# Attention scores and maxima as products over 64 rows, issued in couples on the two row halves of TensorE's array

## What is computed

```
q = split_heads(x @ Wq + bq, 16); k = split_heads(x @ Wk + bk, 16); v = split_heads(x @ Wv + bv, 16)
pattern = jnp.einsum('bhid,bhjd->bhij', k, q) * scale      # 2048 x 2048 for each of 2 x 16 heads
prob = jax.nn.softmax(pattern, axis=-2)                    # over the keys i, for each query j
out = jnp.einsum('bhis,bhid->bhsd', prob, v)
```

## Time and profile before

| | |
|---|---|
| median of 3 runs | 4837.88 us (4835.5 to 4839.3) |
| profiled execution, its own time | 4833.63 us |
| span of the profiled execution | 4831.8 us |
| TensorE busy | 4504.0 us, 93% of the span |
| VectorE busy | 3447.5 us, 71% |
| GpSimd busy | 2736.8 us, 57% |
| ScalarE busy | 2191.5 us, 45% |

### The profile page before, as it was taken

How to read it: one execution, slowest core, us unless ns; L and a number is a source line. 1 busy time by engine, 2 the same in 40 slices (tenths; PEclk the granted TensorE clock), 3 DMA queues, 4 the chain that set the end, 5 groups by cost and what they waited for, 6 DMA issues and landing times.

```text
span 4831.8 us, 57873 instructions
## 1 busy us (share of the span) xinstructions
PE 4504.0 (93%) x21400; PEld 2750.5 (57%) x21400; DVE 3447.5 (71%) x4562; ACT 2191.5 (45%) x3523; POOL 2736.8 (57%) x1202
## 2 busy tenths in 40 slices
PE   7999999999999999999999999858999896989898
PEld 5555555555555555555555555426777665767575
DVE  6888878878788788787888887465655454566455
ACT  5434444434444444444444444315565443555442
POOL 3666656566555565565565666705666233666432
PEclk9999999999999999999999999979999998999999
DMA  2000000000000000000000000010000100000001
GB/s 65 1 5 4 2 5 1 5 5 1 5 4 2 5 1 5 5 1 5 4 2 5 3 2 2 1 57 1 0 1 1 36 1 18 1 1 1 1 1 35
DMA packets 58327, 36.26 MB, mean 8 GB/s; under 512 B 33684, under 2 KB 56168, under 8 KB 58088
## 3 DMA queue, kind: packets, MB, share of 16 engines
q1 hardware_dynamic: 58088, 33.02, 2.4%
HBM read 28.54 MB, written 4.19 MB: 7 GB/s over the span
## 4 chain that ended last, share of the span: by engine, by line
POOL 48%; issue 26%; PE 11%; DVE 8%; ACT 4%; POOLq 1%; DMA 0%; DVEq 0%; SPq 0%; ACTq 0%
POOL accp L738 36%; POOL lp L760 4%; PE psum L1627 3%; POOL accp L734 3%; PE psum L1756 2%; POOL rnorm L750 2%; POOL qk_u L755 2%; PE psum L1769 2%; DVE ssq L1227 1%; ACT lp L941 1%; PE psum L1673 1%; ACT qk_sq L925 1%; DVE qk_w L1239 1%; POOL ug_l L788 1%; DVE lneg L1253 1%
## 5 line engine op out<-in xcount | busy, mean ns | idle before, releaser
L738 POOL TENSOR_TENSOR accp<-accp,prob 128x1024 f32<-128x1024 f32 x640 | 1593.7, 2490 | 712.1 <-ACT prob L895 675.1
L895 ACT ACTIVATE prob<-psum 128x1024 f32<-128x1024 f32 x1024 | 1041.4, 1025 | 1559.6 <-PE psum L1478 1400.0
L1124 DVE TENSOR_REDUCE mx<-psum 128x1 f32<-128x512 f32 x1984 | 1276.3, 684 | 383.9 <-PE psum L1449 338.5
L1489 PE MATMUL psum<-prob,vv 128*64 128x512 f32 x4096 | 991.6, 605 | 0.0
L1477 PE MATMUL psum<-qhh,klh 128*128 128x512 f32 x2048 | 826.1, 403 | 14.0 <-DVE klh L1087 11.8
L1478 PE MATMUL psum<-qlm,kh 65*128 65x512 f32 x2048 | 814.0, 397 | 0.0
L1449 PE MATMUL psum<-klh,qhh 128*128 128x512 f32 x1984 | 710.1, 419 | 30.5 <-DVE mx L1124 27.2
L1449 PEld LDWEIGHTS psum<-klh,qhh 128*128 128x128 f32 x1984 | 346.3, 189 | 430.6 <-DVE mx L1124 272.2
L1489 PEld LDWEIGHTS psum<-prob,vv 128*64 128x64 f32 x4096 | 248.4, 136 | 511.3 <-issue 433.6
L1477 PEld LDWEIGHTS psum<-qhh,klh 128*128 128x128 f32 x2048 | 390.4, 191 | 178.3 <-issue 69.7
L1147 DVE TENSOR_TENSOR accd<-accd,prob 128x1024 f32<-128x1024 f32 x192 | 421.6, 2196 | 22.5 <-ACT prob L895 21.3
(11 more groups left out here) (194 smaller groups left out, 6451.4 us busy)
## 6 DMA issues: line engine op xcount, KB each, us to landing
rot_l<-const_rot SPq DMA_DIRECT2D x2, 2048.0 KB, 8.7
out<-lpT SPq DMA_DIRECT2D x32, 128.0 KB, 1.7
wqkv_l<-L_ffn_wqkv SPq DMA_DIRECT2D x4, 768.0 KB, 9.7
w_l<-L_ffn_w SPq DMA_DIRECT2D x4, 618.0 KB
wqk<-L_attn_Wq SPq DMA_DIRECT2D x32, 64.0 KB, 2.0
wqk<-L_attn_Wk SPq DMA_DIRECT2D x32, 64.0 KB, 2.0
wv_p<-L_attn_Wv SPq DMA_DIRECT2D x16, 128.0 KB, 2.2
wo_p<-L_attn_Wo SPq DMA_DIRECT2D x16, 128.0 KB, 2.0
```

The lines of the kernel that those rows point to most:

```text
L738: pool.tensor_tensor(acc_p[cp][:], first[:], prob[kt % PRING][:], ALU.add).then_inc(pool_sum, 1)
L895: act.activation(prob[t % PRING][:], psum[:, S_BANK + 2 * (t % 2):S_BANK + 2 * (t % 2) + 2, :].rearrange("p a b -> p (a b)"), ACT.Exp, sca ...
L1124: dve.tensor_reduce(mx4[:, j // CHUNKS, j % CHUNKS:j % CHUNKS + 1], ps, AX_X, ALU.max).then_inc(ring_free, 1)
L1489: mm = pe.matmul(psum[j * DH:(j + 1) * DH, O_BANK, :], vv[:, kt, s * DH:(s + 1) * DH], prob[t % PRING][:, j * T:(j + 1) * T], start=(kt == ...
```

## The change

The operands of a head are laid out anew. Of the four chunks of 512 queries or keys, chunks 0 and 2 have their queries in rows 0 to 63 (e = 0), chunks 1 and 3 in rows 64 to 127 (e = 1). `qh` and `ql` (128 x 1024) hold high and low queries, `kh` and `kl` (128 x 2048) high and low keys in both row halves. Three blocks of weights (Wq, Wk, Wq) let one projection over 128 columns put queries above keys or keys above queries.

A step's scores are four couples of products, each couple one product over rows 0 to 63 for the one block of queries and one over rows 64 to 127 for the other: `one`.`nm` (ones in one row, the negated maxima), `kh`.`qh`, `kl`.`qh` and `kh`.`ql`. The maxima are `kh`.`qh` alone, without the low keys, also as a couple: 32 couples in a head in place of 64 products. VectorE still reduces 64 tiles. A couple takes two banks of the ring at once.

The second copy of the high keys is written by ScalarE, in place of its second copy of the high queries; that of the low keys by two transfers on SyncE's queue (`double_low`), for which TensorE waits at the start of the head (`kl_in`). VectorE's copy of the high keys (L1085) is gone. The negated maxima go into `nm` by two transfers. More weights and biases are loaded.

```diff
-            return [-(-RING_MAX * sum(weight[:g + 1]) // sum(weight)) for g in range(GROUPS)]
+            return [-(-COUPLES * sum(weight[:g + 1]) // sum(weight)) for g in range(GROUPS)]
...
-                tiles = [("max", j) for j in range(done, upto)]
+                couples = [("max", k) for k in range(done, upto)]
+                head = couples[:-1][:1]
+                middle = couples[1:-1]
+                tail = couples[-1:]
                 if g in outs:
-                    tiles += [("out", 2 * (g - 1)), ("out", 2 * (g - 1) + 1)]
+                    tail += [("out", 2 * (g - 1)), ("out", 2 * (g - 1) + 1)]
...
-                    order += tiles[:cut0] + [("scores", 2 * g + 2)] + tiles[cut0:cut1] + [("scores", 2 * g + 3)] + tiles[cut1:]
+                    order += head + [("scores", 2 * g + 2)] + middle + [("scores", 2 * g + 3)] + tail
...
+            def double_low(G, s):
+
+                sp.wait_ge(pj_dve, G * QK_ITEMS + QK_ITEMS)
+                for e in range(2):
+                    to, src = (kl[s][half(o), :].bitcast(F32).rearrange("p (c e n) -> p c e n", e=2, n=T)[:, :, e, :] for o in (e, 1 - e))
+                    sp.dma_start(to, src).then_inc(kl_in[s], 16)
...
-                    act.activation(qhh[s][DH:P, cols], qhh[s][0:DH, cols], ACT.Copy).then_inc(pj_dup, 1)
+                    act.activation(kh[s][q, cols], kh[s][k, cols], ACT.Copy).then_inc(pj_dup, 1)
...
-                dve.tensor_copy(kh1[s][0:DH, cols], klh[s][DH:P, cols])
-                dve.scalar_tensor_tensor(qlm[s][0:DH, cols], ps[0:DH], bqk_h[s][0:DH, 0:1], qhh[s][0:DH, cols], ALU.add, ALU.subtract)
-                dve.scalar_tensor_tensor(klh[s][0:DH, cols], ps[DH:P], bqk_h[s][DH:P, 0:1], klh[s][DH:P, cols], ALU.add, ALU.subtract).then_inc(pj_dve, 1)
+                dve.scalar_tensor_tensor(ql[s][q, pair_cols], ps[q], bqk_h[s][q, e:e + 1], qh[s][q, pair_cols], ALU.add, ALU.subtract)
+                dve.scalar_tensor_tensor(kl[s][k, cols], ps[k], bqk_h[s][k, e:e + 1], kh[s][k, cols], ALU.add, ALU.subtract).then_inc(pj_dve, 1)
...
-            def max_tile(rb, i, j):
-                ps = ring_wait(rb, i)
-                dve.tensor_reduce(mx4[:, j // CHUNKS, j % CHUNKS:j % CHUNKS + 1], ps, AX_X, ALU.max).then_inc(ring_free, 1)
+            def max_couple(rb, r, k):
+                qt, c = divmod(k, CHUNKS)
+                for e in range(2):
+                    ps = ring_wait(rb, r + e)
+                    dve.tensor_reduce(mx4[:, e, qt, c:c + 1], ps, AX_X, ALU.max).then_inc(ring_free, 1)
...
-                pe.matmul(ps, qhh[s][:, qt * P:(qt + 1) * P], klh[s][:, c * T:(c + 1) * T],
-                          start=True, stop=True).then_inc(ring_full, 1)
+            def couple_product(banks, s, k):
+
+                qt, c = divmod(k, CHUNKS)
+                for e in range(2):
+                    mm = pe.matmul(banks[e], qh[s][half(e), qt * P:(qt + 1) * P], kh[s][half(e), c * T:(c + 1) * T], start=True, stop=True)
+                return mm
+
+            def max_couple(rb, r, s, k):
+
+                couple_product([ring_slot(rb, r + e) for e in range(2)], s, k).then_inc(ring_full, 2)
...
-                for j in range(2):
-                    cols = slice((2 * cp + j) * T, (2 * cp + j + 1) * T)
-                    ps = psum[:, S_BANK + 2 * (t % 2) + j, :]
-                    pe.matmul(ps, klh[s][:, keys], qhh[s][:, cols], start=True, stop=False)
-                    mm = pe.matmul(ps, kh1[s][:, keys], qlm[s][:, cols], start=False, stop=True)
+                cols = slice(cp * T, (cp + 1) * T)
+                parts = ((one[:], nm[s]), (kh[s][:, keys], qh[s]), (kl[s][:, keys], qh[s]), (kh[s][:, keys], ql[s]))
+                for n, (left, right) in enumerate(parts):
+                    for e in range(2):
+                        mm = pe.matmul(psum[:, S_BANK + 2 * (t % 2) + e, :], left[half(e)], right[half(e), cols],
+                                       start=(n == 0), stop=(n == len(parts) - 1))
                 mm.then_inc(s_full, 1)
...
-                    pe.wait_ge(mrow, G * 16 + 32)
+                    pe.wait_ge(mrow, G * 32 + 64)
+                    pe.wait_ge(kl_in[s], p * 32 + 32)
```

More of the change, by code:

```diff
@@ L265, in adaln_block @@
         pj_full, pj_hi, pj_dup, pj_dve = sem("pj_full"), sem("pj_hi"), sem("pj_dup"), sem("pj_dve")
+        kl_in = [sem(f"kl_in{s}") for s in range(2)]
         ring_full, ring_free = sem("ring_full"), sem("ring_free")
@@ L355, in places @@
                 return 2 if j == TWINS - 1 else 1
-            return int(kind in ("max", "sum", "out", "proj_v"))
+            if kind == "max":
+                return 2
+            return int(kind in ("sum", "out", "proj_v"))
         def pair_plan(which):
@@ L376, in place, with half, couple_columns @@
             return [r for k, _, r in PLAN[which][hh] if k == kind][-1]
+        def half(e):
+            return slice(e * DH, (e + 1) * DH)
+        def couple_columns(i):
+            return slice(i // 2 * T, (i // 2 + 1) * T)
         def head_index(p, hh):
@@ L635, in _ @@
             pair(ALL_PAIRS - 1, True, PAIRS - 1, None, LAST)
-            sp.wait_ge(mrow, 16 + 16 * HEADS * B)
+            sp.wait_ge(mrow, 32 + 32 * HEADS * B)
+            for s in range(2):
+                sp.wait_ge(kl_in[s], 32 * ALL_PAIRS)
             sp.sem_inc(bar_left, 1)
@@ L701, in _ @@
             for s in range(2):
[L702 to L703 removed]
+                pool.memset(nm[s][:].bitcast(F32), 0.0).then_inc(cst, 1)
+            pool.memset(one[:].bitcast(F32), 0.0).then_inc(cst, 1)
+            pool.wait_ge(cst, 4)
+            for e in range(2):
+                pool.memset(one[e * DH:e * DH + 1, :].bitcast(F32), 1.0).then_inc(cst, 1)
+            pool.wait_ge(cst, 6)
             pool.sem_inc(pool_sum, OFF_POOL)
@@ L1547, in first_maxima @@
                     pe.wait_ge(pm_free, k - 1)
-                qt, c = divmod(2 * k, CHUNKS)
-                for j in range(2):
-                    mm = pe.matmul(psum[:, 4 + 2 * (k % 2) + j, :], qhh[0][:, qt * P:(qt + 1) * P], klh[0][:, (c + j) * T:(c + j + 1) * T],
-                                   start=True, stop=True)
-                mm.then_inc(pm_full, 1)
+                couple_product([psum[:, 4 + 2 * (k % 2) + e, :] for e in range(2)], 0, k).then_inc(pm_full, 1)
             def first_values(i):
```

84 lines of the change are left out of this document (44 added, 40 removed).

## The result

| | before | after |
|---|---|---|
| median of 4 runs | 4836.69 us (4834.45 to 4839.3) | 4791.02 us (4789.22 to 4792.51) |
| span of the profiled execution | 4831.8 us | 4787.1 us |
| first turned maximum (start) | 92.7 us | 97.2 us |
| last turned maximum (start) | 3052.1 us | 3002.6 us |
| from the first to the last | 2959.4 us | 2905.5 us |

The ratio is 0.9905, with an interval of 0.9888 to 0.9922: the change makes the kernel faster by 45.7 us. The sign was forecast and the time lies in the range given, but the gain is 46 us where the sum had 104.

A forecast was written before the change was run, and what follows sets the result against it. TensorE was taken to bound the kernel. Per pair of heads -14.9 + 0.4 + 8.3 - 0.4 = -6.6 us, x 15.5 = -102, with the start -104: median 4734 us (-2.2%), range 4600 to 4800.

The forecast's parts named there:

- the sum: Whole kernel: -6.6 us a pair of heads over 15.5 pairs, -102, and with the start -104 us.
- A couple costs one product: TensorE's maxima and scores: a couple takes 0.233 us, so the maxima save 14.9 us a pair of heads.
- Rivals 3 and 4: TensorE's couples overlap only in part, 5198 us (chance 0.06), or not at all, about 5790 us (0.03).
- the sum of the maxima, shapes and projection: TensorE's work per pair of heads: maxima -14.9 us, changes of shape +0.4, projection -0.4.
- The wait for the ring: Maxima in groups of three behind a VectorE addition: TensorE waits 1.1 us, seven times a pair, 7.7 us.
- some 0.15 in each of 12 such groups, 1.8: Groups of three couples: VectorE needs 1.29 us for two tiles, couples come 1.17 apart; 1.8 us a pair.
- The 0.6 for the output tiles: Output tiles behind a couple wait some 0.15 us in four groups, 0.6 us a pair of heads.
- The pair: Attention, per pair of heads: -14.9 + 0.4 + 8.3 - 0.4 = -6.6 us.
- The start: First head's maxima, paced by VectorE: eight copies of 0.5 us go, half on the path, -2 us.
- Rival 1: Ring in the attention: VectorE keeps up and waits stay as before; 4605 us, chance 0.17.
- Rival 2: Ring in the attention: slowed additions cost 2.2 us each time and eat the gain; 4853 us, chance 0.12.
- The transfers: Doubling of the low keys, 2 x 256 KB a head: hidden by a whole head, cost nothing.

The follow-up runs named there:

- e9: The changed kernel with VectorE's additions over 64 of 1024 columns and its reductions of the maxima over 256 of 512; 4589.8 us.
- e1: The changed kernel with other counts of couples in the groups, so that no group of three follows a VectorE addition; 4700.4 us, ratio 0.9723.
- e2: The changed kernel with VectorE's additions of the probabilities over 64 of 1024 columns; 4664.8 us.
- e4: The changed kernel with each half of a couple of maxima waiting for its own bank of the ring; 4736.6 us, ratio 0.9795.
- e3: The changed kernel with VectorE's reductions of the maxima over the first 256 of 512 columns; 4701.1 us.
- e6: The changed kernel with every couple of the first head's maxima issued twice into the same banks; 4783.5 us.
- e10: The changed kernel with the edits of e1 and e4, and every couple of the first head's maxima issued twice; 4641.2 us, ratio 0.9598.
- e5: The changed kernel with the two transfers that double the low keys issued a second time, TensorE waiting for all four; 4789.4 us.

## Why the prediction was right and wrong

**A couple costs one product: right.** The two products start within 0.01 us (up to 0.06 behind a couple that was released late), couples 0.23 us apart, at the earlier trace rows's price and not at the 0.30 estimated from the Trainium skill (TensorE: Matmul & The Clock Gate, "Measured speedup vs the span model"), whose four-row case is no guide to two halves here. Rivals 3 and 4 fall, and e9 confirms the sum of the maxima, shapes and projection to 0.1 us a pair.

**The wait for the ring: right in place, kind and single size** (1.12 us measured, 1.1 by hand); e1 and e2 remove most of it, by the placing and by the addition ahead, and e4 a third, by letting the halves go apart. Over a pair the large waits are 8.5 us in place of 7.7.

**The mis-sized term is "some 0.15 in each of 12 such groups, 1.8"**. The prediction took the difference of two rates (1.29 us of reductions against 1.17 of TensorE) for the whole delay. The trace showed 0.42 in a group without a large wait and 0.31 beside a large one, so 4.1 us a pair. There is a delay at each of four places, not one: whenever a couple is released late by VectorE, its weights are loaded late too (0.03 us ahead of it in place of 0.24), and the next product comes 0.31 us behind it in place of 0.23. That account of the four places is read from the starts, from the rows of the loads and from e3, in which they shrink; that the loads are the reason was not tried by itself. The 0.6 for the output tiles was right: by their starts they lose about 0.6 a pair.

The pair: -6.6 forecast; +0.8 large waits, +2.3 in the groups of three, makes -3.5, and the stretch gives -53.9 / 15.5 = -3.5. Of the 102 us forecast for the attention 48 went there.

**The start: wrong sign.** -2 forecast, +4.5 measured. VectorE's copies did go, but TensorE, with a couple in place of two products between its small ones, ran at 1.2 GHz for most of 20 us and became the bound there. The prediction's step had VectorE as what paces the first head's maxima, and nothing for TensorE's clock. Up to there the forecast held: TensorE comes to the first of the one-column products 2.7 us earlier than before (61.79 in place of 64.47). Behind that 7.2 us are lost, in the stretch at 1.2 GHz. No run shows what the start takes with its own products and the clock held: e6 and e10 bring it back only with added products, which in e6 cost as much as they gave.

**The rest.** From the last turned maximum to the end before took 4831.8 - 3052.1 = 1779.7 us and takes 1784.5, 4.8 more, nearly all of it in code that is the same: -53.9 + 4.5 + 4.8 is the difference of the spans, -44.7, within rounding. The granted clock over the last 730 us is 0.95 in place of 0.97. In all eleven changed kernels the windowed attention and what follows take 1565.1 to 1568.4 us, in place of 1562.6, at a lower clock (0.954 to 0.959 in place of 0.962). Why it is lower in unchanged code stays open.

**Rival 1** (4605 us, VectorE keeps up) is where the kernel would be with the waits gone, and e9 with 4590 shows that its price was about right. Its condition fails: idle time of VectorE in the mean does not help a couple that needs two of three banks at once. **Rival 2** would have needed 14.9 us of added waits a pair before the change does harm; 11.4 were added (8.5 + 4.1 + 0.6, in place of 1.8), where the forecast had 8.3. So the outcome lies nearly halfway to it. Its reason, additions of over 3 us each time, is not what happened: the mean stayed 2.2. **The transfers** cost nothing, as said (e5).

## What to carry to other kernels

When a unit of work is made coarser (here two banks taken at once from a ring of three), the saving on the engine and the new wait are two separate numbers. Lay the order out group by group for the consumer as well, once with and once without its other work, and price also the groups in which the consumer is only a tenth slower: their small delays show in no wait of the products and came to about half of the large ones (4.1 and 8.5 us a pair). Then place the coarse units away from the consumer's long instructions and let each half wait for its own bank: both cost nothing, and they gave another 142 us where the change alone gave 46. TensorE, whose large products between small ones were halved, also fell to half its clock here (0.51 granted in place of 1.00).

## What the runs showed of the hardware that was not expected

**VectorE's addition and GpSimd's take turns.** GpSimd's instructions around the group above, after:

```profile
953.67 2.37 POOL L770 TENSOR_TENSOR accp<-accp,prob 128x1024 f32<-128x1024 f32 x1 [2.71 <-ACT prob L928]
956.20 3.15 POOL L770 TENSOR_TENSOR accp<-accp,prob 128x1024 f32<-128x1024 f32 x1 [0.16 <-POOL accp L770]
...
1064.36 2.38 POOL L770 TENSOR_TENSOR accp<-accp,prob 128x1024 f32<-128x1024 f32 x1 [0.16 <-POOL accp L770]
```

and VectorE's addition beside the last of them:

```profile
1064.49 3.33 DVE L1182 TENSOR_TENSOR accd<-accd,prob 128x1024 f32<-128x1024 f32 x1
```

The first GpSimd instruction ends at 956.04, VectorE's addition (954.93, 2.19 us) at 957.12, 1.08 later; the third ends at 1066.74, VectorE's at 1067.82, again 1.08 later. And GpSimd's that is issued at 956.20, while the addition still runs, takes 3.15 us in place of 2.37. These are not two chosen cases: of the 192 additions after the change 191 begin beside an instruction of GpSimd and end 1.08 to 1.09 us behind its end; the one that meets none takes 1.23 us in all. So what is above that is standing still. It is why an addition of only 64 columns still takes 1207 ns in the mean (e2), where the shortest takes 249.

The Trainium skill (SBUF — State Buffer, "SBUF: two separate sides") calls the port pair that the two engines share an exclusive lock, held for a whole instruction, when VectorE has two inputs in SBUF; both cases above agree. The reductions read PSUM and keep their 684 ns. The prediction's 2.2 us for an addition was therefore not a cost but a mean of waits, and it moved, to 2685 ns, as soon as e3 changed when the additions fell.

**Halves out of step run at full pace**, as e4 showed: out of step each half still started a product every 0.23 us. A couple is not a unit for the array, only for whoever waits.
